# Cross attention in software-pipelined steps: both norms in one vector chain, folded products for all batches at once, router logits as extra score columns

## The chip, the cores and the metric

One core of one Trainium2 chip runs the whole program in one launch. The metric is device time in microseconds (us). Engines are named as in the profile: PE is TensorE, DVE is VectorE, ACT is ScalarE, POOL is GpSimd, SP is SyncE, whose queue only issues transfers here.

## The reference

A decoder block on x of 4 batches x 1024 tokens x 256 channels: self attention with 16 heads, cross attention to 77 context tokens, and a mixture of 8 experts in which each expert takes its 512 best tokens. The part that changes:

```python
x = x + self_attention(layernorm(x))          # ends in a projection: @ proj_w.T + proj_b
# cross attention, one head of 256, D = 256
kp = ctx @ Wk.T;  vp = ctx @ Wv.T + bv;  qp = layernorm(x) @ Wq.T + bq
probs = softmax(qp @ kp.T / sqrt(D))          # 1024 x 77 in each batch
x = x + probs @ vp @ Wo.T + bo
# experts, on layernorm(x)
xn = z * rsqrt(mean(z * z) + eps) * norm_weight      # z = layernorm(x)
logits = xn @ router_w.T + router_b                  # 8 experts
probs = softmax(logits); gates, idx = top_k(probs.T, 512)
hmid = gelu(xn[idx] @ fc1_w.T + fc1_b); ye = hmid @ fc2_w.T + fc2_b
out = scatter_add(ye * gates) / gate_sums            # and x + out
```

## The kernel before

Four stages run one behind the other, each in a block of its own, and all engines meet between blocks: the projections to q, k and v (`project_qkv`), the self attention (`attend`, some 750 us), the cross attention (`cross_attend`, 951.5 to 1154.3 us of the profile) and routing with the experts (`experts`). No planner sets an order. Every engine has its own program text, and semaphores join them, so each engine does its work strictly as its text has it.

`cross_attend` takes half a batch at a time: 512 tokens, which are 4 tiles of 128 (NT). There are 8 halves, j = 0 to 7. A half passes through stages, written as `at(i, h, stage)`, and step s works on half s in stage 0, s-1 in stage 1 and so on, 11 steps in all:

- Stage 0: SP loads x (`c_x`) and the self attention's output (`c_attT`). POOL adds the bias (`c_xb`, L1053). PE projects (L1171 with `c_wp`), DVE adds (x1, L1084), and takes the first norm's statistics: four BN_STATS (L70), four BN_AGGR (L75), and then a chain of 13 small instructions on 128x4 numbers (L78, `rsqrt` at L59 to L64, L1130), each of which waits for the one before it. ACT normalises (`c_xn`, L991). POOL adds the output's bias ahead of time (`c_x1b`, L1065).
- Stage 1: PE transposes `c_xn` (L1159), ACT takes it (`c_xnT`, L997), and PE makes the scores with keys in which Wq is folded (`c_kq`, L1206). DVE adds the key bias (L1106) and finds the maximum, ACT takes the exponential (L1021), DVE normalises (`c_probs`, L1116), and PE transposes (L1221).
- Stage 2: PE multiplies by values in which Wo is folded (`c_vo`; the profile has it under L1171 too, from the shared helper `product`). DVE adds x1 (x2, L1084 with `c_x1b`), and runs the second norm's statistics with a second chain of 13 (L78, L59 to L64, L1099). ACT makes `c_z` (L991), POOL multiplies by the norm weight (`c_xr`, L1060), and SP stores x2 (L968) and the row (L970).
- Stage 3: PE transposes the row again (L1159 with `c_xr`), ACT takes it (`c_xrT`), PE makes the 8 logits for each token (L1241 with `c_wr`), and DVE adds the router's bias (`logits`, L1144).

Every second step PE also makes the folded keys and values of one batch (L1233, L1249, L1252, L1255). In a record an fp32 matmul stands twice, so a x16 row is 8 matmuls. DVE's order in a step is: residual and statistics of stage 2, scores, softmax, residual and statistics of stage 0, logits. Steps 4 to 7 are a hardware loop of two turns, the others are unrolled.

In `experts` each expert's fc1 weights are split into a leading and a trailing part: ACT copies (L1417), DVE subtracts (L1664, L1703).

## Time and profile before

| what | us |
|---|---|
| median of 3 runs | 1467.3 |
| the 3 runs | 1458.6, 1467.3, 1470.69 |
| the profiled execution's own time | 1462.76 |
| its span, first to last instruction | 1461.1 |
| of it the cross attention's block | 951.5 to 1154.3, 202.8 |
| busy in the whole span: PE, DVE, ACT, POOL | 1187.3, 1094.9, 767.4, 437.2 |

The span leaves out 1.7 us of the execution's time. The block's ends are the first instructions of its engines and the first of the next block. The clock in the profile is the share of full speed (2.4 GHz) granted to PE; it has two levels, 0.5 and 1.0, and values between them are means over a stretch.

### The profile page before, as it was taken

Reading aid. Unit: us, or ns where it says so; the run is one execution under the profiler, and the core shown is the slowest. Engines: PE = TensorE matmul, PEld = TensorE weight load, DVE = VectorE, ACT = ScalarE, POOL = GpSimd, SP = SyncE. Lnnn points to the kernel's source line nnn. Section 1 sums busy time; section 2 is a strip of 40 time slices with the busy share of each in tenths; the row PEclk is TensorE's granted clock in tenths of the full one; section 3 lists DMA queues with packets and bytes.
Section 4 is the critical chain, followed back from the end, with each engine's and each line's share of the span. In section 5 each row is a group of like instructions: output and inputs, shape, how many; then the busy total and the mean of one; then the engine's idle time right before and its main releaser. Section 6 shows DMA issues by size and latency. Waiting matters only on the chain. (4 is left out here: it accounts for less than half of the span.)

```text
span 1461.1 us, 25874 instructions
## 1 busy us (share of the span) xinstructions
PE 1187.3 (81%) x8662; PEld 652.2 (45%) x8662; DVE 1094.9 (75%) x2559; ACT 767.4 (53%) x936; POOL 437.2 (30%) x412
## 2 busy tenths in 40 slices
PE   5867668499999999999999999866977405799995
PEld 3544433133333333333333333355766304688894
DVE  6855568399999889898999999237776486776751
ACT  2321104277877777687778887813334202455552
POOL 5644563121210221101221000123332002467564
PEclk9888857699999999999999999977776556999997
DMA  3154747533313333223333000152331102334532
GB/s 124 57 189 158 187 102 199 111 72 70 63 38 60 74 75 68 44 46 71 75 71 69 19 17 14 22 160 73 107 118 58 32 0 87 90 96 136 131 91 29
DMA packets 80185, 120.64 MB, mean 83 GB/s; under 512 B 22785, under 2 KB 57345, under 8 KB 79041
## 3 DMA queue, kind: packets, MB, share of 16 engines
q1 hardware_dynamic: 64080, 79.24, 18.0%
q0 software_dynamic: 15984, 39.86, 14.5%
q8 instruction: 68, 1.11, 0.3%
q14 instruction: 53, 0.43, 0.1%
HBM read 75.93 MB, written 42.21 MB: 81 GB/s over the span
## 5 line engine op out<-in xcount | busy, mean ns | idle before, releaser
L687 DVE TENSOR_REDUCE b_max_halves<-banks 128x1 f32<-128x512 f32 x1024 | 630.3, 681 | 73.8 <-PE banks L754 73.4
L633 ACT ACTIVATE b_probs<-banks 128x1024 f32<-128x1024 f32 x512 | 520.3, 1026 | 183.7 <-PE banks L806 182.1
L806 PE MATMUL banks<-b_q,b_k 64*128 64x512 f32 x1024 | 393.7, 463 | 49.6 <-DMA b_q<-b_max_rows 43.3
L754 PE MATMUL banks<-b_k,b_q 62*128 62x512 f32 x1024 | 404.0, 477 | 3.2 <-DVE b_max L704 2.1
L776 PE MATMUL banks<-b_probs,b_v 128*32 128x256 f32 (+1 forms) x3840 | 325.7, 412 | 2.2 <-ACT b_out L620 0.3
L806 PEld LDWEIGHTS banks<-b_q,b_k 64*128 64x128 f32 x1024 | 163.1, 188 | 271.3 <-issue 174.7
L462 POOL TENSOR_TENSOR b_att<-b_out,b_rec_spread 128x512 f32<-128x512 f32 x32 | 40.9, 1277 | 576.0 <-DMA b_rec_spread<-reciprocals 576.0
L754 PEld LDWEIGHTS banks<-b_k,b_q 62*128 62x128 f32 x1024 | 167.9, 193 | 35.7 <-DVE b_max_halves L687 31.6
L776 PEld LDWEIGHTS banks<-b_probs,b_v 128*32 128x32 f32 x3840 | 76.3, 108 | 169.1 <-issue 89.7
L1469 POOL DMA_INDIRECT e_x<-rows,d_idx x32 | 52.2, 1631 | 127.7 <-DVE d_wx L1650 64.7
L310 POOL TENSOR_TENSOR a_t<-a_qk,a_sin 128x256 f32<-128x256 f32 x64 | 52.6, 843 | 86.0 <-DVE a_t L262 86.0
L340 PE MATMUL banks<-a_w,a_xnT 128*128 128x512 f32 x128 | 75.5, 722 | 2.7 <-DVE a_v L258 1.4
L1778 PE MATMUL banks<-e_w2h,e_hTh 128*128 128x256 f32 x256 | 73.7, 288 | 0.0
L1778 PE MATMUL banks<-e_w2l,e_hTh 128*128 128x256 f32 x256 | 72.9, 285 | 0.0
L1778 PE MATMUL banks<-e_w2h,e_hTl 128*128 128x256 f32 x256 | 72.9, 285 | 0.0
L1679 DVE TENSOR_TENSOR e_hTl<-e_hT,e_hTh 128x512 fp32r<-128x512 f32 x64 | 43.6, 691 | 38.4 <-ACT e_hT L1445 37.9
L1442 ACT ACTIVATE e_hTh<-banks,e_b 128x512 fp32r<-128x512 f32 x64 | 44.1, 689 | 53.4 <-PE banks L1778 50.5
L217 ACT ACTIVATE a_parts<-banks 128x512 fp32r<-128x512 f32 x32 | 18.8, 594 | 89.4 <-DMA k_stacks<-a_parts 32.9
L271 DVE TENSOR_TENSOR a_parts<-banks,a_parts 128x512 fp32r<-128x512 f32 x32 | 22.0, 687 | 56.6 <-ACT a_parts L217 56.6
L1428 ACT ACTIVATE e_xTh<-banks 128x512 fp32r<-128x512 f32 x16 | 8.7, 595 | 102.5 <-PE banks L1766 102.5
L355 PE MATMUL banks<-ident,a_rot 128*128 128x128 f32 x128 | 23.4, 317 | 43.3 <-POOL a_rot L313 38.3
L1778 PE MATMUL banks<-e_xTh,e_w1h 128*128 128x512 f32 x128 | 53.6, 418 | 2.6 <-DVE e_xTl L1656 2.6
(222 smaller groups left out, 1725.2 us busy)
## 6 DMA issues: line engine op xcount, KB each, us to landing
e_w<-in_w SPq DMA_DIRECT2D x16, 1024.0 KB
v_tiles<-a_v SPq DMA_DIRECT2D x8, 1024.0 KB, 11.9
q_stacks<-a_parts SPq DMA_DIRECT2D x16, 512.0 KB
k_stacks<-a_parts SPq DMA_DIRECT2D x16, 512.0 KB
b_q<-q_stacks POOLq DMA_DIRECT2D x30, 256.0 KB, 6.6
b_k<-k_stacks POOLq DMA_DIRECT2D x30, 256.0 KB, 7.6
b_v<-v_tiles POOLq DMA_DIRECT2D x15, 512.0 KB, 10.2
a_x<-in_x SPq DMA_DIRECT2D x8, 512.0 KB, 4.8
```

The source lines that it names most:

```text
L310: ins = g.tensor_tensor(dst[:, :, :, u], src[:, :, :, 1 - u], ss, ALU.mult)
L340: nc.tensor.matmul(ps[:, 2 + q, :], xnT[:, h, k, P * t:P * t + P], w[:, k, 0:2 * C], start=(k == 0), stop=(k == KC - 1))
L462: g.tensor_tensor(self.att[:, x, :], self.osb[:, x, :], self.rb[:, x, :], ALU.mult).then_inc(self.s_att, 1)
L633: nc.scalar.activation(pr[:, S % NP, u], ps[:, 2 * u:2 * u + 2, :], ACT.Exp, scale=D ** -0.5).then_inc(s_ex[u], 1)
L687: v.tensor_reduce(mxp[:, (k // NB) % 2, s, p, t, kh:kh + 1], ps[:, bank(last), :], AX.X, ALU.max)\
L754: nc.tensor.matmul(ps[:, bank(last), :], qs[g][stack, p, at:at + P], ks[g][stack, p, CH * kh:CH * kh + CH], start=True, stop=True).then_in ...
L776: last = nc.tensor.matmul(ps[VW * j:VW * j + VW, PV, at], vs[hg // 2][:, kt, j, :], pr[:, S % NP, j // 2, j % 2, at], start=(kt == 0), sto ...
L806: return nc.tensor.matmul(ps[:, 2 * u + s, :], ks[g][stack, u, P * kt:P * kt + P], qs[g][stack, u, CH * h:CH * h + CH], start=True, stop=True)
L1442: nc.scalar.activation(hh[:, f, :], ps[:, UP[f % len(UP)], :], ACT.Gelu, bias=b1[:, x, f:f + 1])
L1469: g.indirect_dma_start(xe[:, x, h, :], None, xrow, bass.IndirectOffsetOnAxis(ap=idx[:, n, h:h + 1], axis=0)).then_inc(s_g[x], 16)
L1679: v.tensor_tensor(hl[:, f, :], hf[:, f % NH, :], hh[:, f, :], ALU.subtract).then_inc(s_hl, 1)
L1778: ins = mm(o, a, b, start=(start and m == 0), stop=(stop and m == len(pairs) - 1))
```

## The change

`cross_attend` is written anew, and the norm weight moves into the experts. Part by part:

1. **Steps.** 10 steps instead of 11, all unrolled, no loop registers. Step s has the first norm of half s, the scores of half s-1 and the values of half s-2. The exponential of a half is still made in its score step, but its sums, division and transposes come one step later.
2. **One chain.** DVE does both residuals and both sets of BN_STATS first, then takes the scores, and then runs one chain on 128x8 numbers for the first norm of half s and the second of half s-2. It ends in one semaphore (`s_st`), on which both normalisations of ACT wait.
3. **Folds.** The key and value products are made once with 308 columns for all four batches, ahead of step 1 and, for the values, inside step 1 (`fold_values`). The output bias is folded into the values, so `c_x1b` and its POOL add go. The context comes in one transfer.
4. **Router.** The logits are made from 8 more columns in the scores' product (85 instead of 77 columns) and from a product of the probabilities with `c_vw` (four matmuls of 8 columns in each step), and put together by DVE once at the end (L1130 to L1139). The transposes of `c_xr`, their ACT copies and the POOL multiply by the norm weight go. `c_z` is stored as the row.
5. **Norm weight.** It multiplies the router's weights once, and fc1's weights when they are split: two ACT copies with a scale in place of one, two scalar_tensor_tensor on DVE in place of one subtraction.
6. **Start.** SP issues both halves' loads first, then the last self-attention group's reciprocals, and only then the first expert's weights.

```diff
--- before.py
+++ after.py
...
-            def step(i, h):
...
-            steps(act, step)
...
+            for s in range(NS + 1):
+                if 0 <= s - 1 < J:
+                    j = s - 1
+                    act.wait_ge(s_st, s)
+                    normalise(xn[:, j % 2], x1[:, j % 3], j, 0, s_na)
+                if 0 <= s - 2 < J:
+                    act.wait_ge(s_tp, s - 1)
+                    copy(pT[:], ps[0:SK, 2, :]).then_inc(s_tpe, 1)
+                if 0 <= s - 1 < J:
+                    act.wait_ge(s_tn, s)
+                    for k in range(KC):
+                        last = copy(xnT[:, k, :], ps[:, k, :])
+                    last.then_inc(s_tne, 1)
+                if s == 1:
+                    fold_values()
+                if 0 <= s - 3:
+                    j = s - 3
+                    act.wait_ge(s_st, s)
+                    after(act, s_sr[j % 2], 16 * (j // 2))
+                    normalise(z[:, j % 2], x2[:, j % 2], j + 2, 1, s_nb)
+                if 0 <= s - 1 < J:
+                    j = s - 1
+                    act.wait_ge(s_mx, s)
                     for t in range(NT):
+                        last = nc.scalar.activation(pe_[:, j % 2, t, :], sc[:, j, t, 0:SK], ACT.Exp,
+                                                    bias=mx[:, j % 2, t:t + 1])
                     last.then_inc(s_ex, 1)
...
+            def bias(j):
+                pool.wait_ge(s_xi[j % 2], 16 * (j // 2) + 16)
+                after(pool, s_m1e, 2 * j - 2)
+                g.tensor_tensor(xb[:, j % 2], xs[:, j % 2], bp[:].unsqueeze(1).to_broadcast([P, NT, C]), ALU.add)\
...
+            for s in range(NS):
+                first, second = s < J, 0 <= s - 2
+                if second:
+                    x = s % 2
+                    dve.wait_ge(s_ex, s - 1)
+                    chain(v.tensor_reduce(sm[:, x], pe_[:, x], AX.X, ALU.add))
+                    chain(v.reciprocal(rc[:, x], sm[:, x]))
+                    v.tensor_tensor(pn[:, x], pe_[:, x], rc[:, x].unsqueeze(2).to_broadcast([P, NT, SK]),
+                                    ALU.mult).then_inc(s_pn, 1)
+                if first:
+                    dve.wait_ge(s_xb, s + 1)
+                    residual(s_m1, s_m1e, s, (4, 5), xb[:, s % 2], x1[:, s % 3])
+                    ins = moments(0, x1[:, s % 3])
+                if second:
+                    j = s - 2
+                    after(dve, s_so[j % 2], 16 * (j // 2))
+                    after(dve, s_nb, j - 1)
+                    residual(s_m2, s_m2e, j, (3, 7), x1[:, j % 3], x2[:, j % 2])
+                    ins = moments(1, x2[:, j % 2])
+                chain(ins)
+                if 0 <= s - 1 < J:
+                    j = s - 1
+                    w = SZ if j else SW
+                    dve.wait_ge(s_sc, s)
+                    dve.wait_ge(s_kqe, KC + 1)
+                    v.tensor_tensor(sc[:, j, :, 0:w], ps[:, 6, 0:NT * SZ].rearrange("p (t n) -> p t n", t=NT)[:, :, 0:w],
+                                    cb[:, j // 2, 0:w].unsqueeze(1).to_broadcast([P, NT, w]), ALU.add).then_inc(s_sce, 1)
+                    dve.wait_ge(s_sce, s)
+                    v.tensor_reduce(mx[:, j % 2], sc[:, j, :, 0:SK], AX.X, ALU.max, negate=True).then_inc(s_mx, 1)
+                u = slice(0 if first else NT, 2 * NT if second else NT)
+                for t in range(u.start, u.stop):
+                    ins = v.bn_aggr(mv[:, s, t, :], st[:, t, :])
+                chain(ins)
+                for m in range(2):
+                    if (first, second)[m]:
+                        w = slice(NT * m, NT * m + NT)
+                        ins = v.scalar_tensor_tensor(ve[:, s, w], mv[:, s, w, 1], (1.0, 1.0 + EPS)[m], eps[:, m],
+                                                     ALU.mult, ALU.add)
+                chain(ins)
+                rsqrt(v, chain, rs[:, s, u], ve[:, s, u], tm[:, u])
+                v.scalar_tensor_tensor(nm[:, s, u], mv[:, s, u, 0], -1.0, rs[:, s, u], ALU.mult, ALU.mult)\
+                    .then_inc(s_st, 1)
+            dve.wait_ge(s_sc, J + 1)
+            ones_, twos = slice(0, NT), slice(NT, 2 * NT)
+            v.tensor_copy(sc[:, J, :, SW:SZ], ps[:, 6, 0:NT * SZ].rearrange("p (t n) -> p t n", t=NT)[:, :, SW:SZ])
+            v.tensor_tensor(ru[:], ve[:, 0:J, ones_], rs[:, 0:J, ones_], ALU.mult)
+            chain(v.tensor_tensor(dm[:], mv[:, 0:J, ones_, 0], mv[:, 2:NS, twos, 0], ALU.subtract))
+            over = lambda a: a.unsqueeze(3).to_broadcast([P, J, NT, E])
+            v.tensor_tensor(lb[:], over(dm[:]), csum[:].unsqueeze(1).unsqueeze(1).to_broadcast([P, J, NT, E]), ALU.mult)
+            chain(v.tensor_tensor(la[:], sc[:, 0:J, :, SK:SW], over(ru[:]), ALU.mult))
+            chain(v.tensor_tensor(lb[:], lb[:], sc[:, 1:J + 1, :, SW:SZ], ALU.add))
+            chain(v.tensor_tensor(la[:], la[:], lb[:], ALU.add))
+            chain(v.tensor_tensor(la[:], la[:], over(rs[:, 2:NS, twos]), ALU.mult))
+            v.tensor_tensor(lg[:].rearrange("p (j t) e -> p j t e", t=NT), la[:],
+                            br[:].unsqueeze(1).unsqueeze(1).to_broadcast([P, J, NT, E]), ALU.add)
...
+            def fold_values():
+                pe.wait_ge(s_vpe, KC)
+                for c in range(KC):
+                    product(ps[:, 2 + c, 0:ALLK], [(wo[:, k, P * c:P * c + P], vp[:, k, :]) for k in range(KC)])\
+                        .then_inc(s_vt, 1)
...
-                nc.scalar.activation(w1h[:], w1[:], ACT.Copy).then_inc(s_w1h, 1)
+                for k in range(KC):
+                    last = nc.scalar.activation(w1h[:, k, :], w1[:, k, :], ACT.Copy, scale=nw[:, k:k + 1])
+                last.then_inc(s_w1h, 1)
...
+            def lower_w1():
+                for k in range(KC):
+                    last = v.scalar_tensor_tensor(w1l[:, k, :], w1[:, k, :], nw[:, k:k + 1], w1h[:, k, :],
+                                                  ALU.mult, ALU.subtract)
+                last.then_inc(s_w1l, 1)
...
```

On PE, in the fourth step, this stands before. `c_xr` is the row of half 0, `c_xn` half 2, `c_probs` half 2; `c_wp` works on half 3.

```order
L1171 MATMUL banks<-c_vo,c_probsT 128x256 [waits c_x1_ready,c_probsT_ready]
L1171 MATMUL banks<-c_vo,c_probsT 128x256
L1171 MATMUL banks<-c_vo,c_probsT 128x256 [waits c_x1_ready]
L1171 MATMUL banks<-c_vo,c_probsT 128x256
L1159 MATMUL banks<-ident,c_xr 128x128 [waits c_probsT_ready,c_row_ready]
L1159 MATMUL banks<-ident,c_xn 128x128 [waits c_xnT_ready,c_xn_ready]
L1206 MATMUL banks<-c_kq,c_xnT 128x77 [waits c_scores_taken,c_folded_taken,c_xnT_ready]
L1171 MATMUL banks<-c_wp,c_attT 128x256 [waits c_x2_ready,c_att_in1]
L1221 MATMUL banks<-ident,c_probs 77x128 [waits c_rowsT_ready,c_dve_step3]
L1241 MATMUL banks<-c_wr,c_xrT 128x8 [waits c_rowsT_ready]
```

And on PE in one step after the change, from its first transposes to its projection:

```order
L1202 MATMUL banks<-ident,c_probs 77x128 [waits c_probsT_ready,c_probs_ready]
L1213 MATMUL banks<-ident,c_xn 128x128 [waits c_xnT_ready,c_xn_ready]
L1148 MATMUL banks<-c_vo,c_probsT 128x256 [waits c_x2_ready,c_probsT_ready]
L1148 MATMUL banks<-c_vo,c_probsT 128x256
L1148 MATMUL banks<-c_vo,c_probsT 128x256 [waits c_x2_ready]
L1148 MATMUL banks<-c_vo,c_probsT 128x256
L1148 MATMUL banks<-c_vw,c_probsT 128x8 [waits c_scores_taken]
L1148 MATMUL banks<-c_kqw,c_xnT 128x85 [waits c_scores_taken,c_xnT_ready]
L1148 MATMUL banks<-c_wp,c_attT 128x256 [waits c_x1_ready,c_att_in0]
```

The values' product and its small partner now stand between the transposes of `c_xn` and the scores, and the projection is last and works on the half of the next step.

On DVE a step reads so after the change, without the inner part of the chain:

```order
L1090 TENSOR_REDUCE c_sum<-c_exp 128x4 [waits c_exp_ready]
L1092 TENSOR_TENSOR c_probs<-c_exp,c_rec 128x308 [waits c_dve_step]
L1075 TENSOR_TENSOR c_x<-banks,c_xb 128x512 [waits c_projection,c_x_biased]
L1082 BN_STATS c_st<-c_x 128x6 [waits c_x1_ready]
L1075 TENSOR_TENSOR c_x<-banks,c_x 128x512 [waits c_value_product,c_z_ready,c_out_stored0]
L1082 BN_STATS c_st<-c_x 128x6 [waits c_x2_ready]
L1110 TENSOR_TENSOR c_scores<-banks,c_cb 128x372 [waits c_folded_taken,c_score_product,c_dve_step]
L1113 TENSOR_REDUCE c_max<-c_scores 128x4 [waits c_scores_taken]
L1116 BN_AGGR c_mv<-c_st 128x2 x8
L59 TENSOR_SCALAR c_tm<-c_ve 128x8 [waits c_dve_step]
L1125 SCALAR_TENSOR_TENSOR c_nm<-c_mv,c_rs 128x8 [waits c_dve_step]
```

Before, the scores' take stood between two chains of four columns; now it stands ahead of the only one, and behind both residuals.

## Rows read from the trace of the kernel before

**Rows 1.** The page: the clock granted to TensorE in 40 slices of the span.

```profile
PEclk9888857699999999999999999977776556999997
```

**Rows 2.** Busy time by stretch: length, PE, PEld, DVE, ACT, POOL, PEclk, DMA.

```profile
951.50:1154.30 202.80, 150.95 (x736) 129.77 (x736) 128.73 (x455) 65.91 (x148) 57.54 (x26) 0.71 0.31 98
...
1062.00:1083.00 21.00, 15.36 (x78) 12.54 (x78) 16.65 (x61) 7.89 (x18) 7.03 (x3) 0.76 0.34 104
```

**Rows 3.** The take of the scores, from its tile: durations, first and last start.

```profile
L1106 DVE TENSOR_TENSOR c_scores<-banks,c_cb x8: 478/479/480, 978.6 to 1125.4; 128x308 f32<-128x308 f32 x8
```

**Rows 4.** Waits of the stage, 951 to 1156 us: who waited for whom, us, times, longest.

```profile
ACT c_xn L991 <- DVE c_nm L1130: 44.8, 8, 7.6
...
DVE c_scores L1106 <- PE banks L1206: 21.5, 7, 8.2
```

**Rows 5.** Groups of the stage: busy us, mean ns of one, idle before.

```profile
L1171 PE MATMUL banks<-c_wp,c_attT 128*128 128x256 f32 x128 | 42.8, 508 | 8.4 <-DMA c_attT<-attended 8.4
...
L1206 PE MATMUL banks<-c_kq,c_xnT 128*128 (+1 forms) x128 | 24.7, 370 | 9.9 <-ACT c_xnT L997 9.9
...
L70 DVE BATCH_NORM_STATS2 c_st<-c_x 128x6 f32<-128x256 f32 x64 | 22.5, 414 | 0.5
L1171 PE MATMUL banks<-c_vo,c_probsT 77*128 77x256 f32 (+1 forms) x64 | 19.8, 463 | 0.7 <-ACT c_probsT L1026 0.7
...
L1241 PE MATMUL banks<-c_wr,c_xrT 128*128 128x8 f32 x128 | 18.3, 279 | 2.3 <-ACT c_xrT L997 2.3
...
L1159 PE MATMUL banks<-ident,c_xn 128*128 128x128 f32 x64 | 13.1, 370 | 14.4 <-ACT c_xn L991 14.3
...
L1221 PE MATMUL banks<-ident,c_probs 128*77 128x128 f32 x32 | 5.6, 301 | 6.4 <-DVE c_probs L1116 6.3
...
L63 DVE TENSOR_TENSOR c_tm<-c_tm,c_rs 128x4 f32<-128x4 f32 x24 | 3.9, 163 | 1.1 <-DVE c_tm L62 0.3
```

**Rows 6.** Timeline of PE: start us, us, instruction, count, idle before.

```profile
955.24 6.62 PE L1171 MATMUL banks<-c_wp,c_attT 128*128 128x256 f32 x16 [8.40 <-DMA c_attT<-attended]
...
1058.70 1.04 PE L1159 MATMUL banks<-ident,c_xn 128*128 128x128 f32 x8
1061.01 2.05 PE L1206 MATMUL banks<-c_kq,c_xnT 128*128 x16 [1.26 <-ACT c_xnT L997]
1062.89 3.66 PE L1171 MATMUL banks<-c_wp,c_attT 128*128 128x256 f32 x16
...
1112.19 1.97 PE L1171 MATMUL banks<-c_vo,c_probsT 77*128 77x256 f32 x8
...
1121.65 3.70 PE L1206 MATMUL banks<-c_kq,c_xnT 128*128 128x77 f32 x16 [1.18 <-ACT c_xnT L997]
...
1133.59 3.76 PE L1171 MATMUL banks<-c_vo,c_probsT 77*128 77x256 f32 x8
```

**Rows 7.** The same view of ACT, one step.

```profile
1014.66 2.07 ACT L991 ACTIVATE c_xn<-c_x,c_nm,c_rs 128x256 f32<-128x256 f32 x4 [4.75 <-DVE c_nm L1130]
1017.92 1.09 ACT L997 ACTIVATE c_xnT<-banks 128x512 f32<-128x512 f32 x2 [1.18 <-PE banks L1159]
```

**Rows 8.** The same view of DVE and POOL, around 965 us.

```profile
964.97 2.35 POOL L1053 TENSOR_TENSOR c_xb<-c_x,c_bp 128x1024 f32<-128x1024 f32 x1
965.08 2.27 DVE L59 TENSOR_SCALAR c_tm<-c_ve 128x4 int32<-128x4 int32 x1
```

**Rows 9.** The same view of DVE, the end of the stage.

```profile
1153.86 0.19 DVE L1144 TENSOR_TENSOR logits<-banks,c_br 128x32 f32<-128x32 f32 x1 [11.24 <-PE banks L1241]
```

**Rows 10.** The same view of DVE, the next expert's start.

```profile
1282.96 2.29 DVE L1703 TENSOR_TENSOR e_w1l<-e_w,e_w1h 128x2048 fp32r<-128x2048 f32 x1 [0.42 <-ACT e_w1h L1417]
...
1290.48 1.29 DVE L1656 TENSOR_TENSOR e_xTl<-banks,e_xTh 128x512 fp32r<-128x512 f32 x2 [1.93 <-ACT e_xTh L1428]
```

**Rows 11.** Busy time by stretch around transposes alone.

```profile
1076.70:1080.70 4.00, 3.90 (x16) 3.13 (x16) 3.75 (x17) 2.02 (x4) 0.00 (x0) 0.51 0.38 131
1081.00:1084.00 3.00, 1.92 (x17) 1.93 (x18) 1.13 (x7) 3.00 (x7) 0.00 (x0) 1.00 0.00 0
```

514 lines of the change are left out of this document (212 added, 302 removed).

## The prediction

> **What bounds the kernel now.** The change is in one block and in how fc1's weights are split, so I read the block first. The windows give its length, 202.8 us, and who is busy in it [rows 2]: PE 151, DVE 129, ACT 66, POOL 58. No engine is full, PE is granted 0.71 of its clock, and the page's row of clocks shows the same dip, the longest in the kernel [rows 1]. So the block is a cycle of waits. Its period is in the scores' take: 8 takes from 978.6 to 1125.4, seven steps of 21.0 us [rows 3]. The waits name the cycle [rows 4]: ACT's normalising waits 44.8 us in all for DVE's last chain instruction, and DVE's score take waits 21.5 us for PE. The cycle is chain, normalise, transpose, scores, softmax, and then the chains again, two in each step, one behind the other on DVE. All of it is serial and none of it is large.
>
> Two taxes lie on it. PE at the low clock level takes about twice as long: scores 3.70 against 2.05 us, the values' product 3.76 against 1.97, the projection 6.62 against 3.66 [rows 6]. And while POOL runs an add of 2.35 us, a DVE instruction of 0.17 us can take 2.27 [rows 8]; the 24 POOL adds of the block offer 24 chances.
>
> **The new cycle, worked out.** I follow one steady step from one end of the chain to the next. Behind the chain, ACT normalises in 2.07 us [rows 7]. PE transposes: 1.04 us at the high level [rows 6], 1.95 at the low (16 transposes kept it busy for 3.90 us [rows 11]), and 13.1 / 8 = 1.64 on the mean of the block [rows 5]. ACT's copy of 1.09 us [rows 7] runs beside the values' product. That product now stands ahead of the scores and is on the path: 1.97 high, 3.76 low [rows 6], 19.8 / 8 = 2.48 mean [rows 5]. Then the four matmuls of 8 columns with `c_vw`, half of the old logits' 18.3 / 8 = 2.29: 1.14 mean, and by the ratio of the levels 0.9 high and 1.8 low. Then the scores: 2.05, 3.70 [rows 6], mean 3.09 [rows 5]; 85 columns for 77 add nothing at the mean and at most a tenth at the low level. DVE's tail comes last: take and maximum at 0.48 each [rows 3], 1.1 with handoffs; eight aggregates, which I put at 0.8 (no row of their own here; small ones cost 0.16 [rows 5], and these overlap); and 14 small instructions at 0.163 [rows 5] and some 0.035 of handoff, 2.8. That is 4.7. With 0.2 to 0.3 us for the handoffs between engines:
> - PE always high: 2.07 + 1.04 + 1.97 + 0.9 + 2.05 + 4.7 + 0.25 = 13.0 us.
> - PE at the block's own means: 2.07 + 1.64 + 2.48 + 1.14 + 3.09 + 4.7 + 0.25 = 15.4 us.
> - PE always low: 2.07 + 1.95 + 3.76 + 1.8 + 3.70 + 4.7 + 0.25 = 18.2 us, but here PE itself is fuller than that: 6.62 + 3.70 + 3.76 + 1.95 + 1.8 + about 1.1 for the probabilities' transposes = 18.9 to 19.0 us.
>
> Does everything else fit beside it? DVE's softmax end, two residuals and eight BN_STATS are 1.25 + 2.8 + 22.5 / 8 = 2.8, in all 6.9 us [rows 3, 5], and they run while ACT, PE and ACT bring the next scores, 8 us at the high level: hidden. The projection follows the scores on PE and is done 3.66 to 5.35 us later, beside DVE's tail and softmax end (5.9 us): hidden, except at the low level, where PE is the bound. POOL has one add in each step in place of three; it starts when x has landed and the residual two steps back is done, so early in a step, and the chain is late in it. I take the 2.3 us stall as gone; if it stays, it costs up to 8 x 2.3 = 18 us. SP's loads of half s+2 stand behind the stores of step s-1, and have a whole step to land.
>
> **The start.** PE starts at 955.2 [rows 6], behind a transfer, and will again, with 315 KB of context in place of a quarter of it. A matmul of 308 columns costs 308/256 of the projection's eighth: 0.55 high, 1.0 low, so each set of four is 2.2 to 4.0 us. Three sets, the key bias, the row sums and two projections keep PE until about 972, but the first chain ends beside it, at 968 to 971. Step 1 is another cycle. Inside it stand the folded values: a fourth set, eight transposes, 8 tiny products, each with an ACT copy between, about 7.5 us at the high level. The projection of half 2 and the exponential of half 0 wait behind them, so step 2 takes 17 to 22 us. I get the end of step 2's chain at 998 (high), 1009 (means), 1024 (low).
>
> **The end.** Seven more steps follow. Five are whole. Step 8 has no projection and four columns in its chain, 0.5 us less. Step 9 has no scores: softmax, transposes, values, residual, statistics, chain, 9.8 to 10.5 us (12 low). Then either ACT's last normalising (2.07) with its store and landing, some 3.5, or the logits' sum on DVE, eight instructions on 256 numbers at about 0.43: 5.8 us for the later one. Before, the block ended at 1153.86 + 0.19 and a barrier [rows 9].
> - High: 998 + 5 x 13.0 + 12.5 + 9.8 + 5.8 = 1091, a gain of 63.
> - Means: 1009 + 5 x 15.5 + 14.9 + 10.5 + 5.8 = 1118, a gain of 36.
> - Low: 1024 + 5 x 19.0 + 18 + 12 + 5.8 = 1155, a loss of 1.
>
> **Where between them.** The means belong to a PE that was busy 151 of 203 us [rows 2]. In the new step it has 14.4 us of work at those means in 15.5. Its clock before rose in stretches of dense work and fell behind waits and light products, so a denser step should see more of the high level, while the 8-column products stay. I take steps of 14.5 us, an estimate between 13.0 and 15.5 and nearer to the means, because the sum leaves out what it can't see: end at 1107, gain 47.
>
> **The experts.** fc1's split is two instructions of half the size in place of one, so at most a few tenths more for each expert. DVE's subtraction ends at 1285.25, and the next thing that PE waits for there, the trailing rows, ends at 1291.8 [rows 10]. Cost: nothing. With the cover gone it would be 8 x 0.2 = 1.6 us. The rest of the kernel is untouched.
>
> So the profiled execution goes from 1462.8 to 1416. The median of the runs stands 4.5 us above that execution; I move it by the same 47, to **1420**.
>
> **The rivals.**
> - *PE stays high nearly throughout.* For it: without a wait of more than some 2 us before the transposes, nothing interrupts it. Against it: the 8-column products and that wait remain. 1467 - 63 = 1404.
> - *The clock stays as it is.* For it: scores, small products and transposes follow one another as before, and a busy PE was low in the old block too (window 1062 to 1083: busy 15.4 of 21, clock 0.76 [rows 2]). 1467 - 36 = 1431.
> - *POOL's add meets the chain after all.* One stall of 2.3 us in each step, on top of the forecast: 1438. It would show in the durations of L59 and L60.
> - *The pipeline does nothing, only the chain pays.* If a new wait ties the steps together, what is left is one chain less: 13 instructions at 0.2, 8 x 2.6 = 21 us, and few stalls: 1444.
> - *Slower: PE falls to the low level and becomes the bound.* Its place is the head of each step: behind the projection PE waits for the chain, and what then comes are 12 transposes and light products. If these never lift the clock, the projection runs low as well, a step is 19.4 us with 85 columns at 4.1, and the block ends at 1158, 4 us later than now: 1471. It decides from a mean step of 18.9 us. Against it: in the stretch of 1076.7 to 1080.7, PE did 16 transposes and nothing else at a clock of 0.51, and the stretch that follows shows 1.00 [rows 11]. The page "TensorE: Matmul & The Clock Gate" of the Trainium skill (Part 4, PE-mode transpose) says the opposite: the high level doesn't engage for transposes. By that rule this rival would be the likeliest; the trace here disagrees.
>
> **How the numbers follow.** Forecast (1410 to 1427) 0.45; high clock 0.17; clock as now 0.2; stall 0.06; chain only 0.05; low clock 0.04; anything else 0.03, of it 0.02 slower than all these. A range of 1400 to 1441 holds the first three with their spread and part of the fourth. One per cent, 14.7 us, is about what a measurement of this kernel can tell from no change: faster by more means below 1452.6, which all but the last two cases are. Faster 0.93, same 0.05, slower 0.02.
>
> **What would show it.** Right: the scores' take (L1110) repeats every 14 to 15 us; the block ends near 1107; PE's clock in it is near 0.8 or above; L59 and L60 take 0.17 us nearly always; ACT's normalising still waits for DVE's chain, and DVE's score take for PE. Step 2 is the longest, with `fold_values` ahead of it. The experts' part keeps its length. Wrong: a period above 16 or below 13.5; a clock of 0.7; the first chain after 975; or an experts' part that is some us longer, if the scaled split is slower than I think or the first gather comes at another point.

## The result: 1400.3 us in place of 1466.5

The changed kernel takes 1400.3 us in the median of four runs (1393.1 to 1404.3), the kernel before 1466.5 in the same session (1458.6 to 1470.7). The ratio is 0.956, with a 95% interval from 0.952 to 0.960. The forecast was 1420, so the gain of 66 us is 19 more than the 47 forecast.

The profiled execution took 1393.1 us with a span of 1391.4; it is the fastest of the four. The page's engines and clocks, to be read against [rows 1]. The block fills the 28th to 31st of the 40 slices: its clocks are now 9, 9, 8 and 6, the last with steps 8 and 9.

```profile
PE   4867658399999999989999999997876016999994
...
PEclk9988965699999999999999999999986556999997
```

The windows of the block (first transfer issued to the first instruction of the next block; length, PE, PEld, DVE, ACT, POOL, PEclk, DMA share, GB/s) and of one steady step, to be read against [rows 2]:

```profile
943.66:1085.10 141.44, 102.94 (x544) 87.93 (x544) 92.25 (x354) 59.40 (x133) 20.41 (x11) 0.84 0.43 140
1008.95:1022.64 13.69, 11.29 (x62) 9.84 (x61) 10.24 (x40) 6.70 (x15) 2.35 (x1) 0.88 0.47 153
```

The block went from 203.0 us (951.45 to 1154.40) to 141.4. PE's work fell from 151 to 103 us, DVE's from 129 to 92, POOL's from 58 to 20. Outside the block the span was 1258.1 and is 1250.0. That code is unchanged but for the split of fc1, and the difference lies ahead of the block, which starts 7.8 us earlier. Part of it is scatter and part seems not to be: the five profiles of the kernel before and its variants have a remainder of 1255.7 to 1260.5 us (mean 1258.5), the nine of the changed kernel and its variants 1247.9 to 1257.0 (mean 1252.2). Some 6 us thus go with the changed program outside the block, and no run shows why. The experts take 306.3 us, before 306.7. The block is worth 61.5 us between these two executions.

The take of the scores, from its tile [rows 3], and the waits of the block [rows 4]:

```profile
L1110 DVE TENSOR_TENSOR c_scores<-banks,c_cb x8: 512/546/546, 968.2 to 1063.7; 128x372 f32<-128x372 f32 x7, 128x340 f32<-128x340 f32 x1
```

```profile
ACT c_exp L1031 <- DVE c_max L1113: 23.7, 7, 4.5
...
DVE c_x L1075 <- PE banks L1148: 21.5, 14, 4.8
PE banks L1202 <- DVE c_probs L1092: 21.4, 7, 5.5
ACT c_xn L973 <- DVE c_nm L1125: 14.3, 7, 2.5
```

Eight takes from 968.2 to 1063.7: the spacings are 14.62, 12.43 and five times 13.69, where it was 21.0. As expected, ACT's normalising waits for the chain, 14.3 us in place of 44.8, and ACT's exponential for the maximum. New at this size are PE's wait for the probabilities, at the head of each step (21.4 us, 6.3 before), and DVE's wait for PE ahead of its residuals (21.5, 6.5 before). The take's wait for the scores, 21.5 us before, has shrunk to 4.0 us, and the profile puts it down to DVE's own statistics. The groups, by line, engine, operation and tile [rows 5]:

```profile
L1148 PE MATMUL banks<-c_wp,c_attT 128*128 128x256 f32 x128 | 29.3, 382 | 0.3 <-ACT c_vw L968 0.3
...
L1148 PE MATMUL banks<-c_vo,c_probsT 77*128 77x256 f32 x64 | 21.7, 499 | 0.7 <-ACT c_probsT L968 0.7
...
L1148 PE MATMUL banks<-c_kqw,c_xnT 128*128 128x85 f32 x128 | 16.0, 278 | 1.2 <-ACT c_xnT L968 1.2
...
L1213 PE MATMUL banks<-ident,c_xn 128*128 128x128 f32 x64 | 12.7, 366 | 1.9 <-ACT c_xn L973 1.9
...
L1202 PE MATMUL banks<-ident,c_probs 128*77 128x128 f32 x32 | 6.2, 324 | 21.4 <-DVE c_probs L1092 21.4
...
L59 DVE TENSOR_SCALAR c_tm<-c_ve 128x8 int32<-128x8 int32 (+1 forms) x10 | 1.7, 171 | 0.3
```

The projection takes 29.3 us for the same 128 matmuls that took 42.8, and the scores 16.0 for 24.7 with 85 columns in place of 77: both are at the high level nearly always. The transposes of `c_xn` (12.7, before 13.1) and the values' product (21.7, before 19.8) are not. L59 takes 0.17 us, where single ones took 2.27 [rows 8]. One step on PE's timeline shows why (start, us, idle before; [rows 6]):

```profile
1014.40 0.66 PE L1202 MATMUL banks<-ident,c_probs 128*77 128x128 f32 x4 [2.06 <-DVE c_probs L1092]
1015.40 1.87 PE L1213 MATMUL banks<-ident,c_xn 128*128 128x128 f32 x8 [0.34 <-ACT c_xn L973]
1017.07 2.83 PE L1148 MATMUL banks<-c_vo,c_probsT 77*128 77x256 f32 x8
1019.74 0.95 PE L1148 MATMUL banks<-c_vw,c_probsT 77*128 77x8 f32 x8
1020.55 2.00 PE L1148 MATMUL banks<-c_kqw,c_xnT 128*128 128x85 f32 x16
1022.38 0.85 PE L1148 MATMUL banks<-c_wp,c_attT 128*128 128x256 f32 x3
```

PE has nothing to do for 2.06 us at the step's head. The clock falls behind this wait, a little later than its end: the probabilities' transposes still run at 0.66 us, those of `c_xn` take 1.87 where 1.09 is the high level, and the values' product 2.83 where 1.89 is; then it is back. By the granted clock (0.88 of 13.69 us) it is low for 3.3 us in each step, and the two groups lose 1.7. Not every such wait does this. In the step with the spacing of 12.43 PE waited longer and stayed high:

```profile
988.71 0.66 PE L1202 MATMUL banks<-ident,c_probs 128*77 128x128 f32 x4 [2.47 <-DVE c_probs L1092]
...
990.64 1.89 PE L1148 MATMUL banks<-c_vo,c_probsT 77*128 77x256 f32 x8
```

The 1.3 us between this spacing and the others are the clock. On DVE:

```profile
1008.95 0.55 DVE L1110 TENSOR_TENSOR c_scores<-banks,c_cb 128x372 f32<-128x372 f32 x1 [0.57 <-DVE c_st L1082]
...
1013.07 0.17 DVE L1125 SCALAR_TENSOR_TENSOR c_nm<-c_mv,c_rs 128x8 f32<-128x8 f32 x1
...
1019.12 1.51 DVE L1075 TENSOR_TENSOR c_x<-banks,c_x 128x512 f32<-128x512 f32 x2 [2.13 <-PE banks L1148]
...
1022.64 0.55 DVE L1110 TENSOR_TENSOR c_scores<-banks,c_cb 128x372 f32<-128x372 f32 x1 [0.57 <-DVE c_st L1082]
```

From the take to the chain's end it is 4.3 us. Behind the chain the path goes through ACT (2.07), the transposes, the values' product, that with `c_vw` and the scores, which end at 1022.55, to the next take. A second path is nearly as long: from the values' product to the second residual, for which DVE waits 2.13 us, and its statistics, which end 0.57 us ahead of the take.

### The profile page after: what moved, and what is told of

It reads as the page before. It is cut to its first block and busy times, and to the rows that moved or that the text cites. A ratio compares the mean times of both kernels' runs of the same rounds, so it can differ in the third digit from the quotient of the medians.

```text
span 1391.4 us, 25052 instructions
## 1 busy us (share of the span) xinstructions
PE 1133.5 (81%) x8470; PEld 608.8 (44%) x8470; DVE 1060.0 (76%) x2466; ACT 762.4 (55%) x929; POOL 390.9 (28%) x396
## 5 line engine op out<-in xcount | busy, mean ns | idle before, releaser
L462 POOL TENSOR_TENSOR b_att<-b_out,b_rec_spread 128x512 f32<-128x512 f32 x32 | 40.8, 1276 | 575.2 <-DMA b_rec_spread<-reciprocals 575.2
L1458 POOL DMA_INDIRECT e_x<-rows,d_idx x32 | 43.9, 1373 | 130.3 <-DVE d_wx L1639 66.1
L340 PE MATMUL banks<-a_w,a_xnT 128*128 128x512 f32 x128 | 72.1, 694 | 2.7 <-DVE a_v L258 1.4
L355 PE MATMUL banks<-ident,a_rot 128*128 128x128 f32 x128 | 22.9, 313 | 45.3 <-POOL a_rot L313 39.3
## 6 DMA issues: line engine op xcount, KB each, us to landing
e_w<-in_w SPq DMA_DIRECT2D x16, 1024.0 KB, 10.1
```

What stands on the lines that cost most here:

```text
L340: nc.tensor.matmul(ps[:, 2 + q, :], xnT[:, h, k, P * t:P * t + P], w[:, k, 0:2 * C], start=(k == 0), stop=(k == KC - 1))
L462: g.tensor_tensor(self.att[:, x, :], self.osb[:, x, :], self.rb[:, x, :], ALU.mult).then_inc(self.s_att, 1)
L1458: g.indirect_dma_start(xe[:, x, h, :], None, xrow, bass.IndirectOffsetOnAxis(ap=idx[:, n, h:h + 1], axis=0)).then_inc(s_g[x], 16)
```

## The experiments

All lengths of the block below are taken alike, from the first transfer issued to the next block's first instruction on DVE, in the profiled execution. Where two small numbers differ, that column says more than the median, since the rest of the kernel scatters by some 12 us; but each length is from one execution. The four variants of the kernel before leave out parts of the computation: they price these parts and can't be used.

| kernel | median us | ratio to before, 95% | block us | PE clock in it |
|---|---|---|---|---|
| before | 1462 to 1466 | 1 | 203.0 | 0.71 |
| before, two POOL operations out | 1443.9 | 0.979 to 0.991 | 183.3 | 0.74 |
| before, the row's PE and ACT work out | 1460.4 | 0.995 to 1.002 | 200.3 | 0.70 |
| before, context's products once | 1465.9 | 0.998 to 1.004 | 204.0 | 0.68 |
| before, all three | 1443.7 | 0.982 to 0.992 | 181.4 | 0.67 |
| changed | 1400.3 | 0.952 to 0.960 | 141.4 | 0.84 |
| changed, two chains | 1424.5 | 0.965 to 0.976 | 164.4 | 0.74 |
| changed, two POOL adds more | 1438.1 | 0.973 to 0.984 | 190.8 | 0.69 |
| changed, part of the row's PE and ACT work back | 1429.9 | 0.970 to 0.981 | 177.0 | 0.71 |
| changed, late products | 1393.0 | 0.946 to 0.953 | 137.5 | 0.82 |
| changed, fill | 1390.0 | 0.945 to 0.952 | 137.8 | 0.86 |
| changed, fill in all waits | 1387.4 | 0.945 to 0.952 | 130.1 | 0.95 |
| changed, late products and fill | 1388.3 | 0.943 to 0.953 | 131.4 | 0.92 |
| the same with more fill | 1383.0 | 0.943 to 0.951 | 130.3 | 0.92 |

### The chain taken apart again

```diff
-                rsqrt(v, chain, rs[:, s, u], ve[:, s, u], tm[:, u])
-                v.scalar_tensor_tensor(nm[:, s, u], mv[:, s, u, 0], -1.0, rs[:, s, u], ALU.mult, ALU.mult)\
-                    .then_inc(s_st, 1)
                 for m in range(2):
                     if (first, second)[m]:
...
+                        u = slice(NT * m, NT * m + NT)
...
+                        rsqrt(v, chain, rs[:, s, u], ve[:, s, u], tm[:, u])
...
+                ins.then_inc(s_st, 1)
```

> The changed kernel (1400.3 us) with the one chain of a step, on 128x8 tiles, taken apart again into two chains on 128x4 tiles, one behind the other; nothing else is moved, ACT still waits for the last of both. It adds 12 small instructions (ve's wait, eleven of rsqrt less none, nm) in each of the six steps that have both norms. Theory (the chain is on the path, each instruction costs its 0.165 us and a handoff of 0.035): 12 x 0.2 = 2.4 us a step, the take of the scores (L1110) repeats every 16.1 us in place of 13.7, and the kernel takes 6 x 2.4 = 14 us more: 1415. Rival 1 (the step is set by PE, the chain has slack): under 1 us a step, under 1406. Rival 2 (PE's longer wait at the head of the step also costs it its clock for longer): more than 3 us a step, over 1418.

It took 24 us more, the block 23.0, over the mark set for the second rival. The twelve instructions cost what was put: the first `c_nm` starts at 1014.39, the second at 1016.84, 2.45 us later. That is 14.7 us in six steps. The rest, 8.3 us, is the clock as far as the timeline shows. The takes are 19.3 and 14.3 to 15.6 us apart by turns, and in the long ones PE shows:

```profile
1033.79 1.14 PE L1201 MATMUL banks<-ident,c_probs 128*77 128x128 f32 x4 [4.38 <-DVE c_probs L1092]
...
1036.55 3.62 PE L1147 MATMUL banks<-c_vo,c_probsT 77*128 77x256 f32 x8
...
1041.53 3.69 PE L1147 MATMUL banks<-c_kqw,c_xnT 128*128 128x85 f32 x16
```

The wait at the head has grown to 4.38 us, and now the values' product (3.62) and the scores (3.69) are low too. So 14.7 us on the chain cost 23.0 here, one and a half for each.

### POOL beside the chain

```diff
+            def more(s):
+                pool.wait_ge(s_mx, s)
...
+                for n in range(2):
+                    last = g.tensor_tensor(pd[:, 1 + n], pd[:, 0], bp[:].unsqueeze(1).to_broadcast([P, NT, C]), ALU.add)
```

> The changed kernel with two more wide adds of 2.35 us on POOL in each step (outputs that nobody reads), released by the step's maximum, so that they run beside the chain. Theory (the small instructions of DVE stand still while POOL runs such an add, as the 2.27 us for one of them in the kernel before suggests): one or two stalls of about 2.2 us in each of eight steps, L59 to L62 show instructions of over 2 us, and the kernel takes 18 to 35 us more: 1418 to 1435. Rival (the stall of before was a rare meeting, and an add of 2.35 us beside the chain costs it nothing): no instruction of the chain over 0.5 us, time within 3 us of 1400.

The median rose by 38 us and the block by 49.4, more than the theory's upper end of 35. The two differ in part because the profiled execution, 1447.3 us, was the slowest of four. DVE's and POOL's timelines in one step:

```profile
1049.56 0.63 DVE L1129 BATCH_NORM_AGGREGATE c_mv<-c_st 128x2 f32<-128x6 f32 x8
1050.22 1.94 DVE L1134 SCALAR_TENSOR_TENSOR c_ve<-c_mv,c_eps 128x4 f32<-128x4 f32 x2
1052.20 2.20 DVE L59 TENSOR_SCALAR c_tm<-c_ve 128x8 int32<-128x8 int32 x1
1054.43 2.26 DVE L60 TENSOR_SCALAR c_rs<-c_tm 128x8 int32<-128x8 int32 x1
1056.73 0.17 DVE L62 SCALAR_TENSOR_TENSOR c_tm<-c_rs,c_ve 128x8 f32<-128x8 f32 x1
```

```profile
1049.72 4.65 POOL L1054 TENSOR_TENSOR c_pool_more<-c_pool_more,c_bp 128x1024 f32<-128x1024 f32 x2 [12.74 <-DVE c_max L1126]
1054.33 2.33 POOL L1046 TENSOR_TENSOR c_xb<-c_x,c_bp 128x1024 f32<-128x1024 f32 x1
```

Three adds run back to back, to 1052.0, 1054.4 and 1056.7. Each time one instruction of the chain stands until the add that runs has ended, 1.94, 2.20 and 2.26 us in place of 0.2; the next one meets the next add. The eight aggregates, beside the first add, take their 0.63 us as always. The Trainium skill says which may meet ("SBUF — State Buffer", Who interferes with whom): a `tensor_scalar`, where it runs in a mode that uses both ports, or an instruction with two SBUF inputs shares ports with GpSimd, and whoever issues first keeps them for the whole instruction; one with a single SBUF input outside those modes doesn't. The trace agrees in these rows: L59 and L60 are `tensor_scalar`, `c_ve` has two inputs, the aggregates have one. By the groups L59, `c_ve` and L60 took 16.0, 14.2 and 10.1 us in the block where 1.7, 2.5 and 1.7 would do, 34 us. The rest of the 49.4 goes with a lower clock, 0.69: PE was busy 121.1 us with the work that took 102.9.

### POOL's part alone, in the kernel before

```diff
-                    g.tensor_tensor(xr[:, q], z[:, q], wide(nw), ALU.mult).then_inc(s_xr, 1)
...
-                    g.tensor_tensor(x1b[:, q], x1[:, q], wide(bo), ALU.add).then_inc(s_x1b, 1)
```

> One part alone, in the kernel before (1466 us): two of POOL's three wide operations in each step are taken away. It leaves out the sum of x1 with the output bias and the product of the row with the norm's weight; the second residual reads x1, and the row's store and transposes read c_z. Everything else stays as in the kernel before. In that kernel's trace the small DVE instructions that stand still beside POOL are longer than their neighbours by 22.9 us in all (L59 12.1 us for 16 where 2.7 would do, L60 3.5 for 1.4, the max's scaling 5.9 for 1.3, ve 6.1 for 2.6, nm 3.4 for 1.3, the probabilities 5.1 for 3.9). Theory: this is on the path, and the shorter waits keep PE's clock up as well: 18 to 28 us less, 1438 to 1448, with no L59 over 0.5 us. Rival (most of those stalls are covered by PE's slower work): under 8 us, over 1458.

The block is 19.7 us shorter and the ratio 0.985, within the theory. The groups of the kernel before and of this one:

```profile
L59 DVE TENSOR_SCALAR c_tm<-c_ve 128x4 int32<-128x4 int32 x16 | 12.1, 759 | 0.6
...
L1110 DVE TENSOR_SCALAR c_max<-c_max 128x4 f32<-128x4 f32 x8 | 5.9, 735 | 0.3
```

```profile
L59 DVE TENSOR_SCALAR c_tm<-c_ve 128x4 int32<-128x4 int32 x16 | 2.7, 170 | 0.5
...
L1099 DVE TENSOR_SCALAR c_max<-c_max 128x4 f32<-128x4 f32 x8 | 1.4, 171 | 0.3
```

The forecast named the stall and spoke of 24 chances; this is about what they cost, nearly a third of the whole gain. Not all of the 19.7 is stalls: at the end of the block PE had waited 5.03 us for POOL's product of the last row, and waits 2.50 us without it, so 2.5 us are that operation's own time.

### The row's part and the context's part, in the kernel before

```diff
-                    take(xrT, 2, s_tre)
...
-                    transposes(2, xr, q, s_tr)
...
-                            last = mm(ps[:, 3, E * t:E * t + E], xrT[:, k, P * t:P * t + P], wr[:, k, :],
-                                      start=(k == 0), stop=(k == KC - 1))
```

> One part alone, in the kernel before (1466 us): the router's logits leave PE and ACT. It leaves out the transposes of the rows (8 in a step), ACT's two copies and the eight products of 8 columns per half (18.3 us of PE in all, and about 13 for the transposes); the logits are made from x2's first columns instead. POOL's product with the norm's weight and the rows' stores stay. Theory (PE is on the path in a step only between DVE's waits, and the row's part stands ahead of the transposes of c_xn and behind those of the probabilities): about half of PE's 31 us counts, 12 to 18 us less: 1448 to 1454. Rival 1 (PE's work there is all in its waits): under 4 us. Rival 2 (the path was PE's order, all of it counts and the clock is higher as well): over 28 us, under 1438.

```diff
-                if (a := at(i, h, 0)) and h == 0:
+                if (a := at(i, h, 0)) and h == 0 and isinstance(a[0], int) and a[0] == 0:
```

> One part alone, in the kernel before (1466 us): the products of the context (K, V, and what is folded of them) are made for the first batch only, and DVE copies them to the places of all four batches. It leaves out those of the other three batches, so that it shows what their 3 x 18 matmuls, with a wait for ACT between, cost where they stood, at the end of each second step. Theory (they stand behind the step's other work on PE and meet the wait for the chain, so only their overhang counts): 1 to 2 us a batch, 3 to 6 us less: 1460 to 1463. Rival (the loop is a cycle in which PE's order counts): 3 x 4.5 = 13 us less, 1453.

> The kernel before with all three parts left out that were left out one at a time: two of POOL's wide operations a step, the rows' transposes, copies and products of 8 columns, and the context's products of batches 1 to 3. It leaves out the same parts of the computation as those three runs. What stays is the two chains one behind the other and the order of the steps. One at a time they gave 22, 6 and 0 us. Theory (DVE's serial work and its place in the cycle are the path, PE's work stands in waits): the sum or a little more, 1435 to 1442, so that some 40 us to the changed kernel belong to the one chain and the new order. Rival (each of the three hid the others' gain, and together they free the cycle): under 1425, and the one chain is worth little.

The first left out 28.8 us of PE's work (151.0 to 122.2) and won 2.7 us of block, less than the 4 us of its first rival: the theory that half of it counts is wrong. The second left out 10.7 us and won nothing, less than its theory's 3 to 6. All three together, with 112 us of PE's work left of 151, end at 181.4, as POOL's part alone within 2 us. PE only waits longer (33.4 us for `c_xn`, 14.3 before) at a lower clock, 0.67; how much of the saved work the clock took back isn't shown. So in the old order the path was DVE's two chains and what is tied to them, and 40.0 us from there to the changed kernel belong to the one chain and the new order of the steps. The split chain above gives back 23.0 of these. The other 17 are put down to the order of the steps for want of another candidate; no run has the old order with one chain.

### The row's work put back into the changed kernel

```diff
+                    for k in range(KC):
+                        last = copy(zT[:, k, :], ps[:, k, :])
...
+                            product(ps[:, 6, 4 * SZ + E * t:4 * SZ + E * t + E],
+                                    [(zT[:, k, P * t:P * t + P], wrn[:, k, :]) for k in range(KC)])
...
+                            last = mm(ps[:, k, P * t:P * t + P], z[:, (s - 4) % 2, t, P * k:P * k + P], ident[:],
+                                      is_transpose=True, start=True, stop=True)
```

> The changed kernel with the row's work of the kernel before put back on PE and ACT, its results read by nobody: from step 4 on eight transposes of c_z behind the projection, two copies on ACT behind the exponential, and from step 5 on eight products of 8 columns ahead of the scores. Theory (in the new order too PE has room in its wait at the head of the step, and the transposes there even keep its clock up; only the products ahead of the scores are on the path): 4 x 0.95 us more and about 5 x 1.7 less by the clock, 1394 to 1402. Rival 1 (the work is on the path): 5 x (1.0 + 1.1 + 0.95) = 15 us more, 1415. Rival 2 (ACT's copies hold up its normalising behind the chain): 1 us a step more, 1405 to 1408, with ACT's normalising waiting for no one.

It took 30 us more, the block 35.6: the theory is plainly wrong, and each rival too small. It isn't the whole of the row's work: the transposes stand in six steps, the products of 8 columns in four (5 to 8), not the five of the expectation. In steps 5 to 7 the takes are 22 us apart, in step 8 20.4. PE and ACT in one step:

```profile
1045.15 1.97 PE L1222 MATMUL banks<-ident,c_xn 128*128 128x128 f32 x8 [1.89 <-ACT c_xn L975]
1046.92 3.62 PE L1156 MATMUL banks<-c_vo,c_probsT 77*128 77x256 f32 x8
1050.33 1.71 PE L1156 MATMUL banks<-c_vw,c_probsT 77*128 77x8 f32 x8
1051.89 3.56 PE L1156 MATMUL banks<-c_wrn,c_zT 128*128 128x8 f32 x16
1055.31 3.69 PE L1156 MATMUL banks<-c_kqw,c_xnT 128*128 128x85 f32 x16
```

```profile
1042.07 1.09 ACT L970 ACTIVATE c_zT<-banks 128x512 f32<-128x512 f32 x2 [2.72 <-PE banks L1264]
1043.04 2.06 ACT L975 ACTIVATE c_xn<-c_x,c_nm,c_rs 128x256 f32<-128x256 f32 x4
```

The chain ended at 1041.44, but ACT's copies of the row stand ahead of its normalising, which starts at 1043.04: 1.6 us. From there all of PE's work on the path is low: the eight products of 8 columns 3.56 us, the values 3.62 for 2.83, `c_vw` 1.71 for 0.95, the scores 3.69 for 2.00. 1.6 + 3.6 + 0.8 + 0.8 + 1.7 = 8.5, the whole difference to 13.7. The work that was worth 3 us in the old order costs 36 here, with even a part of it, in this placement; another might cost less, which wasn't tried. It is what the router's logits as score columns spare the new order.

### PE's wait at the head: late products, and fill

```diff
+                if 0 <= s - 3:
+                    pe.wait_ge(s_sce, s - 1)
+                    row_part(s - 3, SW)
                 if 0 <= s - 2 < J:
                     pe.wait_ge(s_pn, s - 1)
...
-                    pe.wait_ge(s_sce, j + 1)
-                    for t in range(NT):
-                        last = product(ps[:, 6, at(t) + SW:at(t) + SZ], [(pT[:, P * t:P * t + P], vw[:, j // 2, :])])
```

> The changed kernel with the four products of 8 columns (probabilities by c_vw) moved off the path: from ahead of the scores to the head of the next step, where PE waits 2.06 us for the probabilities; the logits' sum then reads two slots further on. Theory A (what stands ahead of the scores on PE is on the path): each step is shorter by the products' 0.95 us, the take repeats every 12.7 us, 8 x 0.95 = 7.6 us less: 1393. Theory B (light products in the wait at the head also keep PE's clock up or bring it up sooner): up to 1 us more a step, down to 1386. Rival (the take waits for DVE's BN_STATS, not for PE, so nothing is won until those are done): under 2 us in all, 1398 to 1401.

```diff
+                if 3 <= s:
+                    pe.wait_ge(s_tpe, s - 2)
+                    for _ in range(8):
+                        product(ps[:, 2, 0:P], [(ident[:], ident[:])])
                 if 0 <= s - 2 < J:
                     pe.wait_ge(s_pn, s - 1)
```

> The changed kernel with eight more products of 128 columns (identity by identity, into the bank of the probabilities' transposes, read by nobody) at the head of steps 3 to 9, where PE waits 2.06 us for the probabilities; by the projection's 3.65 us for 2048 columns they take 1.8 us. Theory (that wait is what PE's clock falls in, and the transposes and the values' product behind it pay for it: 1.87 and 2.83 us in place of 1.09 and 1.89): 1.7 us a step less, the take repeats every 12.0 us, 7 x 1.7 = 12 us less: 1388. Rival 1 (the clock falls whatever PE does in the wait): the transposes stay at 1.87 and the time at 1400. Rival 2 (the fill runs past the wait or keeps the clock down by itself): 1400 to 1408.

The late products won 3.9 us of block (median 7.3, as theory A has it). The path through the second residual is only 0.57 us shorter than that through the scores, so the rival's reason holds and 0.95 a step can't be won by the path alone; spacings from 11.48 to 14.87 us mix, by the clock. So the median that theory A named came without its mechanism. The fill did what was expected in the steps with a projection: spacings of 12.01 us, at a clock of 1.00.

```profile
1040.71 1.95 PE L1148 MATMUL banks<-ident 128*128 128x128 f32 x16
1042.94 0.66 PE L1206 MATMUL banks<-ident,c_probs 128*77 128x128 f32 x4 [0.28 <-DVE c_probs L1092]
1043.94 1.09 PE L1217 MATMUL banks<-ident,c_xn 128*128 128x128 f32 x8 [0.33 <-ACT c_xn L973]
1044.87 1.89 PE L1148 MATMUL banks<-c_vo,c_probsT 77*128 77x256 f32 x8
```

The transposes are at 1.09 and the values at 1.89 us, 1.7 less as put. In step 8, which has no projection, the fill covered 2.0 of 5.7 us of wait, and the take came after 16.97 us, 3.3 later than without any fill: PE stayed low from the transposes through the scores (3.69 us). Four steps gained 1.7 us each, step 3, high before as well, 0.4, and step 8 lost 3.3, so the block won only 3.7 us where 12 were put; the profiled execution is also the slowest of six, 1395.0 for a median of 1390.0. Three kernels followed from this.

> The changed kernel with fill alone: eight products in steps 3 to 7 as in the first run with fill (1390), and 20 in steps 8 and 9, where PE waits 5.5 us. Theory: step 8 goes from 17.0 to 12 us, step 9 gains 3 us by its high clock, the rest stays at 12.0: 7 us less, 1383, and the late products are then worth at most 0.5 us a step. Rival (long fills run into a lower clock by themselves, as 18 products of 5.9 us in one step did): step 8 or 9 gains nothing, 1387 to 1390.

> The changed kernel with both: the products with c_vw at the head of the next step, and behind them as much fill as PE's wait there holds, three products of 128 columns in steps 3 to 7 (0.7 us) and 18 (4.4 us) in steps 8 and 9, which have no projection. Theory: with PE at its high level throughout, DVE becomes the bound: its own work in a step is 11.3 to 11.5 us (in the run with the late products the take repeated after 11.48 us twice), so 0.5 us less than with the fill alone in each of six steps, and step 8, which took 17.0 us with fill that was too short, takes about 12; step 9 runs its transposes, values and row products at the high level, 3 us less. In all 10 us less than with the fill alone: 1380, take every 11.5 us. Rival (the fill in the long waits delays what they wait for, or the clock falls none the less): step 8 stays at 14 to 17 us, 1386 or more.

> The version with late products and fill (1388), with six fill products in steps 3 to 7 in place of three, and 16 in steps 8 and 9 in place of 18. In its trace PE still waited 0.86 us for the probabilities in each step, once its clock fell behind such a wait (transposes of 1.74, values of 2.96 us, a step of 13.2), and step 9's 18 products ran low and 5.9 us long. Three more products take 0.73 us at the high level. Theory (the less PE waits, the more rarely its clock falls): all steps 11.5 us, 2 to 5 us less, 1383 to 1386. Rival (a fill that fills the wait delays the transposes whenever the clock is low, and the fall doesn't come from this wait): 1388 or more.

With 20 products in steps 8 and 9 every spacing from the second on is 12.0 to 12.1, and the block is 130.1 us, 7.6 less than with the first fill. The steps are as its theory has them, while the median, 1387.4, is not: it fell by 2.6 us and lies in the rival's range. Late products with fill give 11.5 us a step, 131.4 and, with six in place of three, 130.3 us of block. In the former the clock fell once behind a wait of 0.86 us, which it had borne four times, and again inside step 9's fill (5.89 us for 18 products, 4.26 in step 8). Its median, 1388.3, misses the theory's 1380 and is in the rival's range, though step 8 took 11.5 us and not 14 to 17. In the latter, at the low end of its theory with 1383.0, the clock fell once too, in step 8's fill. What bounds them now is seen on DVE's timeline of the last:

```profile
1017.32 0.55 DVE L1110 TENSOR_TENSOR c_scores<-banks,c_cb 128x372 f32<-128x372 f32 x1
...
1021.45 0.17 DVE L1125 SCALAR_TENSOR_TENSOR c_nm<-c_mv,c_rs 128x8 f32<-128x8 f32 x1
...
1025.87 1.46 DVE L1075 TENSOR_TENSOR c_x<-banks,c_x 128x512 f32<-128x512 f32 x2 [0.51 <-PE banks L1150]
...
1028.80 0.55 DVE L1110 TENSOR_TENSOR c_scores<-banks,c_cb 128x372 f32<-128x372 f32 x1
```

DVE waits 0.51 us for the values and no more; 11.0 of 11.5 us is its own work with its handoffs. The last version has the lowest median, 1383.0 us, and an interval (0.943 to 0.951) that ends below that of the changed kernel (0.952 to 0.960). It can't be told from the fill alone (1387.4).

## Why the prediction was right, and where its sizes were off

The median, 1400.3 us, lies 0.3 us above the lower end of the range of 1400 to 1441; that it lies inside at all is luck, the mechanism held better than the sizes. Of the signs named, a nearly fixed period came, but 13.69 us lies between the 14 to 15 that were to confirm it and the 13.5 that was to refute it. The block was to end near 1107 and ended at 1085.1, 7.8 us of it by its earlier start.

**The bound.** Right: a cycle of waits with no engine full. The runs on the kernel before show it: with POOL's part out, a cut of PE's work to 112 us moved the block by only 1.9 more.

**The stall.** Right in kind: L59 and L60 take 0.17 us, and the rival in which POOL's add meets the chain didn't come; the add at 1017.87 lies 3 us and more from both chains. Two smaller stalls did come at the start: one L62 of 1.19 us in the first chain, beside the last product of the self attention (L462), and `c_ve` with 0.65 us for two in step 2. What the stalls had cost before was never put into the sum. It was 17 to 20 us.

**The step.** 14.5 us was chosen, 12.43 and 13.69 came. Of the terms, transposes (1.87, mean 1.64) and values (2.83, mean 2.48) were even longer than at the old means, the tail was 4.3 for 4.7, the product with `c_vw` 0.95 for 1.14, and the scores 2.00 where the mean was 3.09. Another 0.5 us is in no term: a group on PE starts before the one ahead of it has ended, by 0.14 to 0.20 us each time. The step that was mis-sized is "Where between them": clock 0.88 in the steady step, not "near 0.8", because the low stretch is 3.3 us and keeps to one place in the step, and scores and projection lie outside it. Five steps took 66.8 us where 72.5 were put: 5.7.

**The start.** This is the largest miss. The forecast implies 53.0 us from the block's start to the end of step 2's chain (1107 less the five steps, 14.0, 10.2 and 5.8). It was 43.9. The first chain was right (18.0 us in, 16.5 to 19.5 put). Step 2 was the longest, as said, but took 15.45 us where 17 to 22 stood, and step 1, from chain to chain, 10.4 us, where the forecast leaves some 13 to 18. The term that was mis-sized is that of `fold_values`: it held PE from 967.96 to 973.27, 5.3 us for 7.5. The sets ran at the high level (2.24 us for four, but for the first with 4.20), yet that is not all: even the sum for the high clock has 46.5 us here. That is 9.1 us.

**The end.** Step 8 took 13.3 us (14.0 put), step 9 11.9 (9.8 to 10.5 put, 12 for the low level). The low level it was, values 3.78 and row products 1.72 behind a wait of 5.16. The tail was 5.6 for 5.8.

47 + 9.1 + 5.7 + 0.7 - 1.7 + 0.2 = 61.0, and 61.5 were measured. The remaining 5 us between this and the medians' 66 lie outside the block, where the changed kernels are some 6 us shorter; the forecast took that part as untouched, and its cause stays open.

**The rivals.** The time is nearest to that of the high clock (1404), but its reason didn't hold: PE waits 2 us in each step and loses its clock for it. That nothing but the chain pays is refuted by the 40 us between the kernel before without the three parts and the changed one, of which the chain is 23. The low level as the bound didn't come, but it is real: with the row's work back a step took 22 us at a clock of 0.66. It came there with waits of up to 2.69 us at the head and more light work behind them, though the transposes of `c_z` before these waits ran high (1.04 us). The rule of the Trainium skill that stood beside this rival ("TensorE: Matmul & The Clock Gate", Part 4), by which the high level doesn't engage for transposes, is neither borne out nor refuted by these runs: behind the same twelve transposes the clock was back within the values' product in one kernel and not before the projection in another, with 2.06 and 4.38 us of wait ahead of them. Against it stand only the rows of the forecast [rows 11].

**The experts**: no cost, as said.

## What to carry to other kernels

Before work is taken from an engine, ask whether the engine waits in that stage anyway: 29 us less of PE's work bought 3 in one order of the steps, and part of the same work cost 36 in the other. Look on the chain of small instructions for the odd one of 2 us among those of 0.17, and sum the excess: it was 22.9 us here, and most of it came off by taking POOL's wide operations away. And price a wait of TensorE together with the clock behind it; where the wait can't go, products that nobody reads, as long as the wait, bought 11 us of block. In a wait of 5.7 us that they filled for 2.0 only, the step took 3.3 us more in the one execution that was profiled.

## What the runs showed of the hardware

- A wide add on POOL (2.35 us) holds one small DVE instruction (`c_ve`, L59 or L60) for as long as it still runs, and three in a row hold three (1.94, 2.20, 2.26 us). Eight aggregates (0.63 us) and the maximum's reduction (0.47 us) that started beside such an add took their usual time.
- TensorE's clock fell behind waits of 2.05 and 2.06 us in the four steady steps that have one, though PE was busy 11.3 of 13.7 us, and the stretch that ran low began 1 us after the wait's end. It did not fall behind a wait of 2.47 us one step earlier. With waits of 0.28 and 0.33 us in 12.0 it stayed at 1.00.
- A wait filled in part need not help: with 2.0 of 5.7 us filled a step took 16.97 us at a clock of 0.60, where 13.69 had stood. Whether the fill did this, in one execution, isn't shown.
- How long it stays low differs much: in the changed kernel 3.3 us of the step; with the chain taken apart, behind 4.38 us of wait, everything from 1033.79 to 1045.0 ran at half speed, though PE hardly paused. The runs don't tell what decides it.
